# Softmax attention: two heads in 64-row tiles of the array, operands in two fp32r parts in place of six bf16 products

## What is computed

```python
qkv = (layernorm(x) @ W_qkv.T).reshape(b, n, 16, 16).transpose(0, 2, 1, 3)
score = softmax(einsum('bhif,bhjf->bhij', qkv, qkv) / 4, axis=-1)
attn = einsum('bhij,bhjf->bihf', score, qkv)
x = x + attn.reshape(b, n, 256) @ W_o.T
```

## Time and profile before

| | |
|---|---|
| median of 3 runs | 3890.41 us (3888.63 to 3891.03) |
| the profiled execution | 3889.07 us |
| its span, first to last instruction | 3887.4 us |
| mean granted clock of PE | 0.974 |

### The profile page before, as it was taken

One profiled execution on the slowest core, in us unless ns is written; L12 is line 12 of the kernel. 1 busy time (PEld: TensorE's weight loads), 2 busy tenths in 40 slices (PEclk: granted clock), 3 DMA queues, 4 the chain that ended last, 5 costly groups with the idle time before them and its releaser, 6 DMA issues. The chain is left out here.

```text
span 3887.4 us, 54302 instructions
## 1 busy us (share of the span) xinstructions
PE 3676.7 (95%) x20930; PEld 2193.3 (56%) x20930; DVE 2808.8 (72%) x5158; ACT 1844.8 (47%) x2480; POOL 653.3 (17%) x556
## 2 busy tenths in 40 slices
PE   6999998999799999899679999999999999998999
PEld 6888886777688888666413333333333333333666
DVE  4545545886454544899478788888888888884998
ACT  3444443222344444222216666666666666666221
POOL 4000003554400000355400000000000000000454
PEclk9999998999899999999859999999999999999999
DMA  3000001000200000000150120211020202000000
GB/s 113 1 1 1 1 1 39 1 1 1 70 1 1 1 1 1 1 1 1 39 59 9 27 32 7 28 14 21 1 34 3 32 10 25 1 1 1 6 17 22
DMA packets 39640, 61.25 MB, mean 16 GB/s; under 512 B 5284, under 2 KB 29912, under 8 KB 39384
## 3 DMA queue, kind: packets, MB, share of 16 engines
q1 hardware_dynamic: 39384, 57.78, 8.1%
HBM read 46.89 MB, written 10.88 MB: 15 GB/s over the span
## 5 line engine op out<-in xcount | busy, mean ns | idle before, releaser
L1645 DVE TENSOR_REDUCE smxp<-psum 128x1 f32<-128x512 f32 x2048 | 1282.3, 683 | 220.1 <-PE psum L1507 219.6
L1603 ACT ACTIVATE spr<-psum 128x1024 f32<-128x1024 f32 x1024 | 996.2, 1021 | 558.0 <-PE psum L1526 555.5
L1507 PE MATMUL psum<-sks,sqs 96*128 96x512 bf16 x2048 | 731.0, 392 | 33.8 <-DMA sqs<-q_parts 30.8
L1526 PE MATMUL psum<-sqs,sks 99*128 99x512 bf16 x2048 | 610.4, 380 | 0.4
L1541 PE MATMUL psum<-spr,sv 128*32 128x512 f32 x4096 | 545.6, 605 | 0.6 <-ACT spr L1603 0.6
L1507 PEld LDWEIGHTS psum<-sks,sqs 96*128 96x128 bf16 x2048 | 164.1, 97 | 612.6 <-issue 378.2
L1526 PEld LDWEIGHTS psum<-sqs,sks 99*128 99x128 bf16 x2048 | 199.6, 98 | 242.7 <-ACT spr L1603 15.2
L1714 POOL CAST smb<-smr 16x128 bf16<-16x128 f32 x32 | 8.9, 279 | 1354.3 <-DVE smr L1664 1354.3
L359 PE MATMUL psum<-w2hi_a,hsa_hi 128*128 128x256 f32 x768 | 217.4, 283 | 16.7 <-DVE hsa_lo L501 16.7
L359 PE MATMUL psum<-w2hi_b,hsb_hi 128*128 128x256 f32 x768 | 217.2, 283 | 10.3 <-DVE hsb_lo L501 10.3
L359 PE MATMUL psum<-w2lo_a,hsa_hi 128*128 128x256 f32 x768 | 217.8, 284 | 0.0
(11 more groups left out here) (290 smaller groups left out, 6751.3 us busy)
## 6 DMA issues: line engine op xcount, KB each, us to landing
sks<-q_parts SPq DMA_DIRECT2D x48, 256.0 KB, 8.9
sqs<-q_parts SPq DMA_DIRECT2D x48, 256.0 KB, 19.6
q_parts<-spart SPq DMA_DIRECT2D x16, 384.0 KB, 2.6
x<-in_L_attn_x_dram SPq DMA_DIRECT2D x8, 512.0 KB, 7.3
rawa<-in_L_ffn_w_dram SPq DMA_DIRECT2D x16, 256.0 KB
rawb<-in_L_ffn_w_dram SPq DMA_DIRECT2D x16, 256.0 KB
out_dram<-x SPq DMA_DIRECT2D x8, 512.0 KB, 2.9
rawa<-in_L_ffn_sw_dram SPq DMA_DIRECT2D x8, 256.0 KB
```

Of the source, the lines that this page charges most:

```text
L1507: e.matmul(bank(what), QS[n % 2][0:KR, h, q0:q0 + P], KS[n % 2][0:KR, h, jc * GW:(jc + 1) * GW], start=True, stop=True).then_inc(*pm_in.up)
L1526: m = e.matmul(st[q % 2][:, i, :], KS[n % 2][0:KM, 2 * hp + i, jt * P:(jt + 1) * P], QS[n % 2][0:KM, 2 * hp + i, ic * GW:(ic + 1) * GW], s ...
L1603: e.activation(PR[j % 2][:, 2 * hp:2 * hp + 2, :], st[hp], ACT.Exp, scale=float(DH) ** -0.5).then_inc(*exp_ok.up)
L1645: e.tensor_reduce(MXP[u % 2][:, r // IC, r % IC:r % IC + 1], bank(what), AX.X, ALU.max).then_inc(*pm_free[use[what] % 3].up)
```

## The change

The parts become two fp32r parts, and the contraction takes three products (first-first, first-second, second-first), 48 rows; two more rows carry two fp32r parts of the maxima. `KS` and `QS` hold two heads at once, one in partitions 0 to 49 and one in 64 to 113, as two pairs of heads (`NPR`) instead of four heads. Each matmul of "max" and "score" names a 64-row tile of the array (`tile_position`). Maxima alternate between the two tiles; the two matmuls of a score pair are in different tiles and different banks. The count of these matmuls and their width stay.

POOL's two operations for each split go (`REST`, `MR`), and the second part is written by the vector engine's subtraction. The two memsets of ones go; a row of 64 ones is made on POOL and copied by eight DMA transfers, for which only the first score waits. Stacks stay at 12 transfers of 256 KB. The maxima go back in two transfers instead of one. Waits and banks are otherwise as before, and `plan()` keeps its order, in another form; small steps put aside come at the end of a step instead of within it.

```diff
-                NPT = 6
+                NPT = 3
                 KR = NPT * DH
-                KM = KR + 3
+                KM = KR + 2
+                HALF = 64
-                KEY = [0, 0, 1, 0, 1, 2]
-                QRY = [0, 1, 0, 2, 1, 0]
+                KEY = [0, 0, 1]
+                QRY = [0, 1, 0]
...
-                KS, QS = ring(scope, "sks", [P, HG, L], 2, BF16), ring(scope, "sqs", [P, HG, L], 2, BF16)
+                KS, QS = ring(scope, "sks", [P, NPR, L], 2, F32R), ring(scope, "sqs", [P, NPR, L], 2, F32R)
...
+                        for jt in range(TB):
+                            j = u * TB + jt
+                            for step in ("max", "low", "max", "high", "max", "pv", "max"):
...
+                            if jt == 0 and u:
+                                yield ("end", u - 1)
+                            if jt == 1 and u:
+                                yield ("tail", u - 1)
+                            if jt > 0:
                                 yield from itertools.islice(aside, 1)
+                            if jt > 1:
                                 yield from itertools.islice(put, 1)
...
+                        e.wait_ge(*fill_ok(1))
+                        for ks in KS:
+                            for pr in range(NPR):
+                                for i in range(2):
+                                    e.dma_start(ks[HALF * i + KR:HALF * i + KM, pr, :].bitcast(F32).rearrange("p (c n) -> p c n", n=HALF),
+                                                ones[:].bitcast(F32).unsqueeze(1).to_broadcast([2, L // HALF, HALF])).then_inc(*ones_in.up)
...
+                                        for i in range(2):
+                                            row = HALF * i + j * DH
+                                            e.dma_start(dst[row:row + DH].bitcast(F32), src[i]).then_inc(*stack_in[n % 2].up)
...
-                                e.matmul(bank(what), QS[n % 2][0:KR, h, q0:q0 + P],
-                                         KS[n % 2][0:KR, h, jc * GW:(jc + 1) * GW], start=True,
-                                         stop=True).then_inc(*pm_in.up)
+                                rows = slice(HALF * a, HALF * a + KR)
+                                e.matmul(bank(what), QS[n % 2][rows, pr, q0:q0 + P],
+                                         KS[n % 2][rows, pr, jc * GW:(jc + 1) * GW], start=True, stop=True,
+                                         tile_position=(HALF * a, 0)).then_inc(*pm_in.up)
...
+                                for a in range(2):
+                                    rows = slice(HALF * a, HALF * a + KM)
+                                    w = e.matmul(st[pr][:, a, :], KS[n % 2][rows, pr, jt * P:(jt + 1) * P],
+                                                 QS[n % 2][rows, pr, ic * GW:(ic + 1) * GW], start=True, stop=True,
+                                                 tile_position=(HALF * a, 0))
+                                w.then_inc(*st_ok.up)
...
-                        e.wait_ge(*fill_ok(2))
+                        e.wait_ge(*fill_ok(1))
...
-                                if n:
-                                    e.wait_ge(*part_ok(n))
-                                e.tensor_tensor(REST[:], bank(what), PART[o][:, 0, :], ALU.subtract).then_inc(
-                                    *pm_free[use[what] % 3].up)
+                                e.tensor_tensor(PART[o][:, 1, :], bank(what), PART[o][:, 0, :].bitcast(F32),
+                                                ALU.subtract).then_inc(*pm_free[use[what] % 3].up)
```

More of the change, by code:

```diff
@@ L1394, in plan @@
                         put = output_steps(u - 1) if u and (u - 1) // IC % NG == NG - 1 else iter(())
[L1395 to L1401, removed]
+                        for jt in range(TB):
+                            j = u * TB + jt
+                            for step in ("max", "low", "max", "high", "max", "pv", "max"):
+                                if step == "low":
+                                    yield ("score", j, 0)
+                                if step == "high":
+                                    yield ("score", j, 1)
+                                if step == "pv" and j:
+                                    yield ("pv", j - 1)
+                                if step == "max":
+                                    if m % MPU == 0 and m <= UNITS * MPU:
+                                        yield ("extremes", m // MPU - 1)
+                                    if m < UNITS * MPU:
+                                        yield ("max", m)
+                                    m += 1
+                            if jt == 0 and u:
[3 more added lines that the diff above has]
+                            if jt > 0:
                                 yield from itertools.islice(aside, 1)
-                            if h > 9 and h % 6 == 4:
+                            if jt > 1:
                                 yield from itertools.islice(put, 1)
[L1405 to L1412, removed]
                         yield from put
@@ L1437, in _ @@
                     def _(e):
-                        for kind, *at in plan():
+                        e.wait_ge(*fill_ok(1))
[4 more added lines that the diff above has]
+                                                ones[:].bitcast(F32).unsqueeze(1).to_broadcast([2, L // HALF, HALF])).then_inc(*ones_in.up)
+                        for what in plan():
+                            kind, *at = what
                             if kind == "parts":
@@ L1459, in _ @@
                                 ic, n = u % IC, u // IC
-                                e.wait_ge(*mb_ok(u + 1))
-                                e.dma_start(maxima[u].rearrange("j r n -> r j n"), MB[u % 2][:]).then_inc(
+                                e.wait_ge(*read(what))
+                                e.dma_start(maxima[u].rearrange("j r n -> r j n"), MB[u % 2][:].bitcast(F32)).then_inc(
                                     *max_in[u % 2].up)
[L1463 to L1466, removed]
+                                e.wait_ge(*max_in[u % 2](3 * (u // 2) + 1))
+                                for i in range(2):
+                                    e.dma_start(QS[n % 2][HALF * i + KR:HALF * i + KM, :, ic * GW:(ic + 1) * GW].bitcast(F32).rearrange(
+                                                    "j r (t n) -> j r t n", n=P),
+                                                maxima[u].rearrange("j (r i t) n -> i j r t n", i=2, t=GT)[i]).then_inc(
+                                        *max_in[u % 2].up)
                     @block.tensor
```

96 lines of the change are left out of this document (35 added, 61 removed).

## The result

The changed kernel takes 3831.41 us (3826.45 to 3835.65, four runs) against 3889.98 us of the kernel before (3888.63 to 3891.03): a ratio of 0.9851, interval 0.9839 to 0.9863. It is 58.6 us faster, or 1.5%; 154 us were forecast. The direction held and the size did not: 95 us of the forecast are missing. The profiled execution lasted 3830.18 us.

What follows compares the result with a forecast made beforehand. The prediction took PE to bound the softmax step, DVE close behind. Steps saving 138 us and the start 16 made 154 us, from 3889.1 to 3735 us; own range 3695 to 3780, 8-in-10 range 3650 to 3875.

Steps and rivals of the forecast that it cites:

- What bounds the kernel: Softmax loop: PE sets the pace at 2.83 us a step, DVE close behind with 2.39 us.
- DVE's floor: Rival: the step falls to DVE's four maxima, 2.39 to 2.45 us; 3652 to 3681 us in all, chance 0.14.
- Tiles together: Maxima and scores in different 64-row tiles overlap in pairs, four slots of 0.235 us for eight matmuls; forecast's chance 0.54.
- in turn: Rival: row tiles don't overlap, each matmul costs PE 0.235 us; step 2.96, 3932 us in all, chance 0.14.
- weak overlap: Rival: matmuls in two row tiles overlap only partly; 3780 to 3880 us in all, chance 0.11.
- Fewer rows give nothing by themselves: Maxima and scores: number and width stay, 8 a step of 512 columns, so cutting rows alone saves nothing.
- The ring of three banks with pv in its middle: Softmax step: the new limit is three banks passing between PE and DVE, with pv between maxima C and D; 2.56 us.
- the step of 2.56: Softmax loop: each step takes 2.56 us instead of 2.84, saving 0.28 x 492 = 138 us.
- The clock at 1.00: Softmax loop: PE's granted clock stays full; the rival, a fall to half, gave 4065 us, chance 0.05.
- Small steps at zero: Loop's transposes and projections: added tiling changes, some 39 us, and PE's slack set to zero together, 25 us kept either way.
- The start: Before the loop: no POOL memsets 12.5 us earlier, no POOL in the splits 3.6 us; together 16 us.
- gain hidden: Rival: another engine, only ACT with 1.94 us, bounds the step and the time stays; chance 0.02.

Runs made afterwards that it cites:

- the one-tile run: Changed kernel with all maxima and scores in the lower 64-row tile, two of four heads computed with the other two's numbers: 5038.1 us, ratio 1.2915.
- After: The changed kernel itself, with fp32r parts in two 64-row tiles, against the kernel before: 3831.41 us, ratio 0.9851.

## Why the prediction came out as it did

**What bounds the kernel: right.** PE's row of matmuls set the pace, and DVE's floor was the next one down (2.38 us in the run with the short pv).

**Tiles together: right.** Two maxima in 0.50 us, two scores in 0.40, and 0.39 us a step lost when one tile did all. The rival "in turn" is out. The measured 3831 us does fall between the 3780 and 3880 us given to a weak overlap, but that is a coincidence of numbers: the overlap of a pair is full, and the time went elsewhere. From D to C it is 1.28 us, where "under 1.25" was to be seen; that distance ends with the wait for C's bank and doesn't measure the pairs.

**Fewer rows give nothing by themselves: right for the step, wrong for the kernel.** The eight matmuls of a step kept their time (47.4 against 47.15 us a unit), but the clock did not keep its level, and each change to work with 128 rows and back became dearer.

**The ring of three banks with pv in its middle: the right mechanism.** Shorten pv and the step falls to the floor; split it and the unit falls by 1.5 us.

**The term that was mis-sized: the step of 2.56.** The forecast took "0.235 + 0.08" from C to pv and "0.44 with the slower fp32r" from a matmul's start to DVE. They measured 0.42 (2503.83 to 2504.25) and 0.53 (2502.55 to 2503.08). Two small things went the other way, the return of a bank with 0.75 in place of 0.79, and pv to D with 0.99. Together 2.69 in place of 2.56: 0.42 + 0.99 + 0.53 + 0.75. What was overlooked is the weight load. An fp32r load of 128 columns is 0.19 us long in its row where bf16 has 0.097, and when PE waits for a bank, the load can't be done ahead, so about 0.10 us of it adds to the matmul (0.34 in place of 0.235 to the next start in the one-tile run). This happens at C and at D, both in the ring. Half the columns took half of it away at both (2.60), and bf16 nearly all (2.49). The rows for it stood in the first layer: the earlier trace rows gave the distance of fp32r matmuls in a stream, where the load is hidden, and I used it for a matmul behind a wait, where it isn't. The Trainium skill, TensorE: Matmul & The Clock Gate, "LDWEIGHTS (loading the stationary operand)", says that a load's time goes by the number of weight columns; the trace agrees that fewer columns are shorter, 0.13 us for 64 against 0.18 to 0.19 for 128, though not in proportion. By its figure, columns / 1.2 ns, 128 would take 107 ns, an estimate that fits the bf16 rows (97) and is short for fp32r. The Trainium skill, same page, "Weight-path perf modes — Fast Weight Load (FWL) and DoubleRow", has a fast load for types other than FP32; that fp32r gets none of it would account for the factor of two, but no run here separates that from the bytes.

The gain of the steps became 0.145 x 492 = 71 us where 138 were reckoned. This is 67 of the 95 us missing.

**The clock at 1.00: wrong.** Its rival was given 0.05. It came partly true, with 65 us at 0.50, which cost 20. My argument against it was a row where PE was busy 7.73 of 9.70 us at full clock. Those were matmuls with 128 rows, of another layer, and they say nothing of 48 rows. Two runs show that PE's busy time isn't what to look at: busy 98.96 of 100 us at 0.50, once with all heads in one tile, once with 48 and 51 rows and no tile named. The section "A second HAM failure mode: psum-queue depth-cycling" of the Trainium skill, TensorE: Matmul & The Clock Gate, which the prediction cites, describes pauses as the cause. After has more pauses (95.3 busy of 100 us at 1.00) and far less time at the half level than either of these runs. For the schedule of before it is shown that the cut from 96 and 99 to 48 and 51 rows brings the half level with PE busy all the time; whether by the rows or by the smaller tile that seems to go with them is open. One thing more stands in the records of every run here: the three full units with projection, where work with 128 rows stands between the steps, are at 1.00 throughout, and in after the first stretch at 0.50 comes at 2293.8, after the last unit with projection (to 2246.8). Such work is not enough by itself, as the units with output projection of the run with fewer rows were at 0.50. What brings each of the short stretches of after is open: filling PE's idle time halved them, half the weight columns left them about as they were, and bf16 parts in the same tiles had two of 3.4 us.

**Small steps at zero: wrong, 13 us.** The forecast let them fall on PE's slack. They stand in a ring that has none at C and D. The five units with projection cost 32.2 us over five plain ones before (267.9 - 5 x 47.15), 35.4 after, and 37.8 with bf16 tiles, where a plain unit is 41.6: the faster the step, the more of them shows. Output units add 4 us in the same way, and the small steps that each of 31 units has ("extremes", "end", "tail") took 0.2 us each of the 2.3 that sixteen steps make: 3 + 4 + 6 = 13 us. Their old places give nothing back (36.0 over plain units). The trace shows what grew: the changes of tiling, which the prediction put at zero. Where four projection matmuls stand between two maxima, it is 1.49 us from one maximum to the next, against 1.09 in the kernel before: 0.20 more ahead of them, 0.10 between the first two, 0.09 behind. Where two transposes stand there, it is 0.79 against 0.46. That is 0.34 to 0.40 us each time, where the prediction had priced 0.23 and set it aside. A full unit with projection has about nine more such places than a plain one, so over 3 us if nothing hid them; 54.84 - 45.05 against 55.19 - 47.15 is 1.7 us. So PE's idle time hid about half, an estimate from these rows; no run took the changes of tiling away by themselves.

**The start: 16 forecast, 19.6 measured.** The first maximum's load moved from 1966.60 to 1947.01, of which 0.7 us came from before the stage:

```profile
1880.28 0.66 ACT L1602 ACTIVATE sxT<-psum 128x256 f32<-128x256 f32 x2 [1.42 <-PE psum L1502]
...
1947.01 0.50 PEld L1527 LDWEIGHTS psum<-sks,sqs 48*128 48x128 f32 x3 [29.72 <-DMA sqs<-q_parts]
```

ACT started 13.4 us earlier (12.5 forecast; I had it start at 1881.2), and the groups of 512 positions follow each other after 9.1 us in place of 10.1, 0.9 less each, as reckoned. The first group gained 1.9. The stack's price of nothing was nearly right: PE's weight load waited 29.72 us for it where it had waited 31.17.

**The account.** 71 from steps, 19.6 from the start, less 20 for the clock and 13 for small steps, is 58 us; 58.6 were measured. The 71 and the 19.6 are read at single places of the traces; the 20 and the 13 are differences between whole units, so that the sum closes shows less than it seems to.

**DVE's floor, weak overlap, gain hidden:** none came about. DVE's idle time before maxima in the loop, 185.6 us before, is still there for the most part (after, 2002 to 3475 us):

```profile
L1663 DVE TENSOR_REDUCE smxp<-psum 128x1 f32<-128x512 f32 x1961 | 1226.6, 682 | 135.1 <-PE psum L1527 133.0
```

## What to carry to other kernels

Matmuls in a stream hide their weight load; one that waits for a bank pays it, so price it there from a row that waited, at the type's own load time. A chain of releases through a small ring of banks has to be added up link by link, and 0.1 us in two links of a step that is walked 492 times was two thirds of the missing gain. When rows of a contraction are cut, look at the granted clock of a run, not at PE's busy time: with half the rows the old schedule ran at the half level for most of the loop. And count the places where matmuls with few rows meet those with 128: each change had a price here, even where no tile was named.

## What the runs showed of the hardware

- Two fp32r matmuls in the two 64-row tiles, to different banks, run together: a pair fills 0.40 us where one fills 0.39.
- With 48 and 51 rows of bf16 and no tile named PE was busy 98.96 of 100 us, and the granted clock was 0.50 from 2421 us to the end of the loop; with 96 and 99 rows it was 1.00.
- Four projection matmuls with 128 rows between two maxima took 1.09 us from maximum to maximum where the maxima had 96 rows, 1.38 where they had 48 rows of bf16 (with a tile named and without), and 1.49 with 48 rows of fp32r.
- A step at the half level takes 5.6 us in the one-tile run against 3.08 at full clock, so most of it nearly doubles. In after it takes 4.16 us (D at 2294.77 and 2298.93) against 2.69: C to pv is 0.72, pv to D 1.86 and D to DVE 0.83, but DVE gives the bank back after 0.75 as at full clock:

```profile
2294.77 0.79 PE L1527 MATMUL psum<-sks,sqs 48*128 48x512 f32 x2
...
2298.93 0.79 PE L1527 MATMUL psum<-sks,sqs 48*128 48x512 f32 x2
```
